# Softplus by ScalarE's own function, three of thirteen products with C from GpSimd to VectorE, and the program written out without loops

## The chip, the cores and the metric

The kernel runs on one core of a Trainium2 chip. The metric is the device time of one execution in microseconds (us). The engines are named as in the profile: PE (TensorE), DVE (VectorE), ACT (ScalarE), POOL (GpSimd) and SP, which only issues DMAs here.

## The reference

Four blocks follow one another on x (8 sequences of 512 positions, width 256): self and cross attention with a gated MLP, four Mamba layers, a cross attention with an MLP, and a last cross attention. The change touches the arithmetic of the Mamba layers alone. There 64 positions of context are put ahead of each sequence, so that 8 x 576 = 4608 positions run through every layer:

```python
def mamba_block(x, ip_w, cw, cb, xp_w, dtp_w, dtp_b, A_log, Dp, op_w):
    xi, z = jnp.split(jnp.einsum('bsd,ed->bse', x, ip_w), 2, axis=-1)      # 512 channels each
    xi = jax.nn.silu(conv4(xi) + cb)
    dt, Bm, Cm = jnp.split(jnp.einsum('bse,fe->bsf', xi, xp_w), [DR_, DR_ + DS_], axis=-1)
    dt = jax.nn.softplus(jnp.einsum('bsr,er->bse', dt, dtp_w) + dtp_b)
    A = -jnp.exp(A_log)                                                    # 512 x 16
    dA = jnp.exp(dt[..., None] * A)
    dBu = dt[..., None] * Bm[:, :, None, :] * xi[..., None]
    h = dA * h_before + dBu                  # along the sequence
    y = sum over the 16 states of (h * Cm)
    y = (y + xi * Dp) * jax.nn.silu(z)
    return jnp.einsum('bse,de->bsd', y, op_w)
```

All of it is float32.

## The kernel before

The activations stay in SBUF in `X`, channels on partitions. The stages run one after another: `self_attention`, cross attention, the gated MLP, `mamba`, a final norm, the second block, `last_attention`. Self attention and the two MLPs go over the eight sequences with `batches`, a hardware loop over seven of them and the last one written out. Each engine has its own loop, and semaphores alone order the engines. In a hardware loop every wait counts up to a number that the engine's sequencer works out in a register first.

`mamba` cuts the 4608 positions into 9 chunks of 512 columns, and so runs 4 x 9 = 36 steps. A hardware loop of two passes holds 18 steps each. A step works on 64 units. A unit is one 128 x 512 tile: 64 channels times two of the 16 states. Two units are a pair, j = 0 to 31, and eight pairs are a quarter k of the step (128 channels). For a pair:

- POOL multiplies dt*x with B for both units at once (L2586, 128 x 1024) into one of six places of `ring`. I call this the feed of pair j. It waits until the pair six before it has been summed by PE.
- ACT computes dA by Exp, one unit an instruction (L2554), into PSUM. Four PSUM banks hold two pairs, so ACT can be at most two pairs ahead of DVE. Before it reuses a place it saves the last column of h (L2173, L2177).
- DVE scans, h = dA*h + dBu, one unit an instruction (L2506).
- The product of h with C is done by DVE, one unit an instruction (`times_c`, L2304), or by POOL for both units (L2591). `BY_POOL` lists which pairs of each quarter are POOL's. POOL does such a product three pairs late: that of pair q follows the feed of pair q + 3.
- PE sums over the states with two products with `fold` (L2450), pair by pair in order.

Between the pairs stands the work that prepares the next step and finishes the last one, at fixed places: `late_pe` and `early_pe` on PE (convolution and projections, L2011, L2029, ...), `late_act` and `early_act` on ACT (copies out of PSUM, two Silu blocks after units 7 and 15, each between two table loads), `times_x` on POOL after the feeds of pairs 26 and 31 (dt*x), the gates on DVE (L2281). The last quarter of a step and the first one of the next hold most of PE's convolution, in order: halves of E1 and E2 at pairs 27 to 31, E3 at pairs 2 and 3. ACT takes E3 after unit 13, and Silu of all four follows after unit 15.

Softplus is not one instruction here. It is max(v, 0) + log(1 + exp(-|v|)), with a correction for rounding: `soft_begin` adds the bias, `soft_magnitude` and `soft_exponent` take Abs and Exp, and for each of four tiles t, `soft_log` writes 1 + e and its logarithm into two PSUM banks, and DVE finishes with three instructions (`soft_rest`, `soft_total`, `soft_finish`). These banks are those of the pairs, so each tile takes a pair's place in the order: after pairs 19, 21, 23 and 25 (`SOFT_AFTER`), 36 places a step in all.

## Time and profile before

| | |
|---|---|
| median of 3 runs | 6814.31 us |
| the runs | 6821.9, 6814.31, 6812.46 us |
| span of the profiled execution, first to last instruction | 6820.7 us |
| PE busy | 6141.5 us, 90% |
| DVE busy | 5101.9 us, 75% |
| POOL busy | 4645.4 us, 68% |
| ACT busy | 3775.4 us, 55% |
| mean granted TensorE clock | 0.946 |

The profile is of one execution, of span 6820.7 us; no other time of it is shown, and the highest of the three runs is 1.2 us above that span. Shares over the whole span mix stages with different limits. The Mamba steps take the stretch from 2057 to 6174 us of it, 60%.

### The profile page before, as it was taken

The page shows a single profiled execution, that of the slowest core. Times are in us where ns is not written, and L with a number is a line of the kernel's source. Part 1 is how long each engine was busy: PE and PEld are TensorE (multiplying, and loading weights), DVE is VectorE, ACT ScalarE, POOL GpSimd, SP SyncE. Part 2 cuts the span into 40 slices and gives each one's busy share as a digit, 9 for nine tenths or more (in the row PEclk, how much of TensorE's full clock was granted, in tenths as well). Part 3 has the DMA queues.
Part 4 walks back from the last instruction along what each step waited for, and adds up shares of the span by engine and source line. Part 5 has one row for each costly group of instructions (what it writes and reads, how often), then busy time and mean ns, then how long its engine had stood idle before and what let it go on. Part 6 is the DMA issues. An engine that isn't in the chain of part 4 may idle for free. (4 is left out here: it accounts for less than half of the span.)

```text
span 6820.7 us, 73597 instructions
## 1 busy us (share of the span) xinstructions
PE 6141.5 (90%) x20586; PEld 2578.2 (38%) x20586; DVE 5101.9 (75%) x5938; ACT 3775.4 (55%) x6915; POOL 4645.4 (68%) x2164
## 2 busy tenths in 40 slices
PE   9999999999999888989898989898888888888898
PEld 4555555444443333323232323232323232323444
DVE  4444555452219999999999999999999999995623
ACT  4444555432236666666666666666666666664432
POOL 3333444223009999999999999999999999993300
PEclk9999999999999898989898989998989999999998
DMA  2000000213003232323232323232333232332000
GB/s 78 0 0 0 0 0 0 83 31 112 0 7 90 68 82 67 95 68 90 61 90 60 93 71 93 60 89 62 87 79 90 63 87 63 87 79 56 5 0 25
DMA packets 228700, 387.50 MB, mean 57 GB/s; under 512 B 46305, under 2 KB 64417, under 8 KB 225937
## 3 DMA queue, kind: packets, MB, share of 16 engines
q1 hardware_dynamic: 228368, 383.75, 23.2%
q8 instruction: 126, 2.06, 0.1%
q14 instruction: 206, 1.68, 0.1%
HBM read 207.14 MB, written 23.40 MB: 34 GB/s over the span
## 5 line engine op out<-in xcount | busy, mean ns | idle before, releaser
L2586 POOL TENSOR_TENSOR work<-work,weights 128x1024 f32<-128x1024 f32 x1152 | 2692.4, 2364 | 15.5 <-PE banks L2450 7.2
L2450 PE MATMUL banks<-work 128*64 128x512 f32 x4608 | 1364.6, 674 | 549.8 <-POOL work L2591 549.3
L2506 DVE TENSOR_TENSOR_SCAN banks<-banks,work 128x512 f32<-128x512 f32 x1368 | 1712.2, 1273 | 41.7 <-ACT banks L2554 41.4
L2554 ACT ACTIVATE banks<-work 128x512 f32<-128x512 f32 x2304 | 1501.2, 680 | 68.6 <-DVE work L2298 43.2
L2506 DVE TENSOR_TENSOR_SCAN work<-banks,work 128x512 f32<-128x512 f32 x936 | 1174.9, 1271 | 98.1 <-ACT banks L2554 70.8
L2591 POOL TENSOR_TENSOR work<-work,weights 128x1024 f32<-128x1024 f32 x468 | 1104.2, 2359 | 159.0 <-ACT work L2173 159.0
L2011 PE MATMUL banks<-work,weights 128*128 128x512 f32 (+31 forms) x3796 | 1142.2, 451 | 3.6 <-DVE work L2271 3.0
L612 POOL TENSOR_TENSOR work<-work 128x1024 f32<-128x1024 f32 x256 | 480.0, 1895 | 743.3 <-DVE work L479 742.8
L2304 DVE TENSOR_TENSOR work<-banks,weights 128x512 f32<-128x512 f32 x1368 | 905.1, 673 | 0.0
L2011 PEld LDWEIGHTS banks<-work,weights 128*128 128x128 f32 x3796 | 634.6, 190 | 601.9 <-issue 523.3
L2450 PEld LDWEIGHTS banks<-work 128*64 128x64 f32 x4608 | 269.3, 144 | 1416.8 <-POOL work L2591 852.6
L2177 ACT ACTIVATE work<-banks 128x2 f32<-128x2 f32 x684 | 117.3, 171 | 1015.5 <-DVE work L2304 1011.3
L562 ACT ACTIVATE work<-banks,work 128x512 f32<-128x512 f32 x512 | 348.1, 690 | 201.1 <-DVE work L473 201.1
L473 DVE TENSOR_REDUCE work<-banks 128x2 f32<-128x1024 f32 x256 | 309.0, 1215 | 104.6 <-PE banks L398 104.6
L2029 PE MATMUL banks<-work,weights 128*128 128x512 f32 x592 | 352.9, 726 | 0.0
L1049 PE MATMUL banks<-work,weights 128*128 128x512 f32 x768 | 340.7, 598 | 11.4 <-ACT work L215 11.4
L463 DVE COPY work<-banks 128x512 f32<-128x512 f32 x256 | 175.9, 687 | 159.9 <-PE banks L388 159.9
L388 PE MATMUL banks<-ident,work 128*128 128x128 f32 x2048 | 277.8, 278 | 8.2 <-DVE work L463 4.7
L388 PEld LDWEIGHTS banks<-ident,work 128*128 128x128 f32 x2048 | 222.1, 141 | 151.7 <-issue 111.1
L398 PE MATMUL banks<-work 64*128 64x512 f32 x1024 | 254.4, 615 | 0.0
L375 PE MATMUL banks<-work 128*64 128x256 f32 x2048 | 247.5, 385 | 0.0
L1597 POOL TENSOR_TENSOR work<-work 128x512 f32<-128x512 f32 x8 | 11.2, 1416 | 322.7 <-ACT work L1712 322.7
(320 smaller groups left out, 7522.7 us busy)
## 6 DMA issues: line engine op xcount, KB each, us to landing
weights<-mamba_bc SPq DMA_DIRECT2D x592, 256.0 KB, 5.0
work<-work SPq DMA_DIRECT2D x1160, 128.0 KB, 2.3
weights<-mamba_taps SPq DMA_DIRECT2D x5, 2048.0 KB, 7.4
weights<-cross_vo SPq DMA_DIRECT2D x16, 512.0 KB, 6.9
mamba_taps<-work SPq DMA_DIRECT2D x4, 2048.0 KB, 6.5
cross_vo<-weights SPq DMA_DIRECT2D x6, 1024.0 KB, 9.2
work<-in_conv_rows SPq DMA_DIRECT2D x16, 256.0 KB, 6.6
out_T<-X SPq DMA_DIRECT2D x8, 512.0 KB, 3.3
```

The source lines that it names most:

```text
L388: mm = e.transpose(core.banks[:, 4 + j, kt * P:(kt + 1) * P], probs[:, 2 * (g % 2) + u, j, kt * P:(kt + 1) * P], core.ident[:])
L562: last = e.activation(probs[:, slot, j, :], core.banks[:, 2 * u + j, :], ACT.Exp, bias=nmax[:, slot, j:j + 1], accum_out=sums[:, slot, j:j ...
L612: e.tensor_tensor(probs[:, slot], probs[:, slot], rsum[:, slot, :].unsqueeze(2).to_broadcast([P, 2, T]), ALU.mult) \
L1049: mm = e.matmul(bank(i), w1[:, k, m * P:(m + 1) * P], normed[:, k, :], start=(k == 0), stop=(k == KD - 1))
L2011: mm = e.matmul(lane[:, a:b], conv_w[j][:, k, m * P:(m + 1) * P], nb[:, k, a + j:b + j], start=(d == 0 and k == 0), stop=(j == 0 and b == ...
L2029: mm = e.matmul(lane, z_w[:, k, m * P:(m + 1) * P], nb[:, k, TAPS - 1:], start=(k == 0), stop=(k == KD - 1))
L2304: last = e.tensor_tensor(ring_pair(n, j)[:, h, :], banks[:, slot_of(i), :], bc[:, j % SP_, 1, :], ALU.mult)
L2450: mm = e.matmul(ybank[k % 2][64 * h:64 * h + 64, :], fold, ring_pair(n, j)[:, h, :], start=False, stop=(a == SP_ - 1))
L2506: e.tensor_tensor_scan(ub if by_pool(j) else da, da, ub, state[:, i:i + 1], ALU.mult, ALU.add).then_inc(scanned, 1)
L2554: e.activation(banks[:, slot_of(i), :], dt_rep[:, k % 2, h, :], ACT.Exp, scale=decay[:, f:f + 1]).then_inc(da_full, 1)
L2586: e.tensor_tensor(ring_pair(n, j), u_rep[:, k % 2], bc[:, a, 0, :].unsqueeze(1).to_broadcast([P, 2, TC]), ALU.mult) \
L2591: e.tensor_tensor(ring_pair(n, q), ring_pair(n, q), bc[:, q % SP_, 1, :].unsqueeze(1).to_broadcast([P, 2, TC]), ALU.mult) \
```

## The change

Softplus becomes one function of ACT. `take_dt` reads PSUM as `soft_begin` did; for the first two tiles it still only adds the bias (after unit 37), for the last two, after unit 45, it applies Softplus at once, and `first_softplus` then turns the first two in one instruction of 1024 columns. A table load stands ahead of the block and one behind it, since Exp is in another table. The Abs, Exp, 1 + e and Ln instructions, the twelve DVE instructions and the four places in the PSUM banks go away. `BY_POOL` gives the products with C of pairs 10, 12, 18 and 22 to DVE and that of pair 11 to POOL: POOL has 10 a step where it had 13. Every hardware loop becomes a Python loop, so each step and each sequence has instructions of its own and constant numbers to wait for.

```diff
 def batches(e, body):
 
-    with e.Fori(0, B - 1) as b:
-        body(b, True)
-    body(B - 1, False)
-
-
...
-BY_POOL = ((0, 5), (0, 2, 4, 6), (0, 2, 4, 6), (0, 2, 4))
+BY_POOL = ((0, 5), (0, 3, 6), (0, 4), (0, 2, 4))
...
-SOFT_AFTER = (19, 21, 23, 25)
-STEP_GROUPS = PAIRS_N + KI
...
-    group_of = lambda j: j + sum(after < j for after in SOFT_AFTER)
-    soft_group = lambda t: SOFT_AFTER[t] + 1 + t
-    slot_of = lambda i: 2 * (group_of(i // 2) % 2) + i % 2
-    soft_slot = lambda t: 2 * (soft_group(t) % 2)
...
+    slot_of = lambda i: 2 * (i // 2 % 2) + i % 2
+    da_full_at = lambda N, i: val(N, UN, i + 1)
...
-    H_OUT, ABS_AT, EXP_AT = (37, 45), (38, 46), (39, 47)
-
-    def soft_begin(e, N, pair):
+    H_OUT = (37, 45)
+
+    def take_dt(e, N, pair, func):
 
         if N[1] >= 0:
             for s in range(2):
                 e.wait_ge(rep_in[s], rep_at(N, 2 * pair))
         ts, tv = ((0, 1), (3, 2))[pair]
         e.wait_ge(ln.s_full, s_at(N, f"H{ts}"))
-        e.activation(dt[:, ts, :], lane_s, ACT.Identity, bias=lv("dt_b", ts)).then_inc(ln.s_free, 1)
+        e.activation(dt[:, ts, :], lane_s, func, bias=lv("dt_b", ts)).then_inc(ln.s_free, 1)
         e.wait_ge(ln.v_full, v_at(N, f"H{tv}"))
-        e.activation(dt[:, tv, :], lane_v, ACT.Identity, bias=lv("dt_b", tv)).then_inc(ln.v_free, 1)
-
...
-        e.activation(u[:, 2 * pair:2 * pair + 2, :], dt[:, 2 * pair:2 * pair + 2, :], ACT.Abs).then_inc(magnitude, 1)
-
...
-        e.activation(u[:, at, :], u[:, at, :], ACT.Exp, scale=-1.0).then_inc(magnitude, 1)
...
-        e.activation(banks[:, b, :], u[:, t, :], ACT.Identity, bias=core.one[:, 0:1]).then_inc(da_full, 1)
-        e.wait_ge(da_full, soft_full_at(N, t, 1))
-        e.activation(banks[:, b + 1, :], banks[:, b, :], ACT.Ln).then_inc(da_full, 1)
...
+        e.activation(dt[:, tv, :], lane_v, func, bias=lv("dt_b", tv)).then_inc(ln.v_free, 1)
+
+    def first_softplus(e, N):
+
+        e.wait_ge(ln.s_free, s_at(N, "H0"))
+        e.wait_ge(ln.v_free, v_at(N, "H1"))
+        e.activation(dt[:, 0:2, :], dt[:, 0:2, :], ACT.Softplus).then_inc(first_dt, 1)
+
+    def slots_free(e, N, n, j):
+
+        M, j = (N, j - 2) if j >= 2 else (previous(N), PAIRS_N + j - 2)
+        m = n if M[1] == N[1] else n - 1
+        if N[1] >= 0 and by_pool(j):
...
-            if i == H_OUT[pair]:
-                soft_begin(e, N, pair)
-            if i == ABS_AT[pair]:
-                soft_magnitude(e, N, pair)
-            if i == EXP_AT[pair]:
-                soft_exponent(e, N, pair)
-        for t in range(KI):
-            if i == 2 * SOFT_AFTER[t] + 1:
-                soft_log(e, N, n, t)
+            if i == H_OUT[pair] and pair == 0:
+                take_dt(e, N, 0, ACT.Identity)
+            if i == H_OUT[pair] and pair == 1:
+                e.preload_act_table_set("softplus")
+                take_dt(e, N, 1, ACT.Softplus)
+                first_softplus(e, N)
+                e.preload_act_table_set("natural_log_exp_and_others")
...
-    def soft_rest(e, N, t):
-
-        e.wait_ge(da_full, soft_full_at(N, t, 2))
-        e.scalar_tensor_tensor(out=u[:, t, :], in0=banks[:, soft_slot(t), :], scalar=1.0, in1=u[:, t, :],
-                               op0=ALU.subtract, op1=ALU.subtract).then_inc(soft, 1)
-
-    def soft_total(e, N, t):
-
-        y = banks[:, soft_slot(t) + 1, :]
-        e.wait_ge(soft, soft_at(N, t, 1))
-        e.scalar_tensor_tensor(out=y, in0=y, scalar=log_1, in1=u[:, t, :], op0=ALU.subtract, op1=ALU.subtract).then_inc(soft, 1)
-
-    def soft_finish(e, N, t):
-
-        e.wait_ge(soft, soft_at(N, t, 2))
-        e.scalar_tensor_tensor(out=dt[:, t, :], in0=dt[:, t, :], scalar=0.0, in1=banks[:, soft_slot(t) + 1, :],
-                               op0=ALU.max, op1=ALU.add).then_inc(soft, 1)
...
-        e.wait_ge(soft, soft_at(N, 2 * pair + 1, 3))
+        if pair == 0:
+            e.wait_ge(first_dt, val(N, 1, 2))
+        else:
+            e.wait_ge(ln.s_free, s_at(N, "H3"))
+            e.wait_ge(ln.v_free, v_at(N, "H2"))
...
-            with e.Fori(0, LAYERS // 2) as l:
+            for l in range(LAYERS // 2):
```

On ACT, in the third quarter of a step, before the change. L2138 and L2140 read PSUM and add the bias, L2146 is Abs, L2152 Exp of the magnitude, L2554 the Exp of one unit; a REGISTER_ALU works out the number that a wait counts to. 1 + e and Ln (L2161, L2163) of each tile follow behind:

```order
L2554 ACTIVATE banks<-work 128x512 x2
L2137 REGISTER_ALU
L2138 ACTIVATE work<-banks,weights 128x512
L2140 ACTIVATE work<-banks,weights 128x512
L2170 REGISTER_ALU
L2554 ACTIVATE banks<-work 128x512
L2146 ACTIVATE work<-work 128x1024
L2554 ACTIVATE banks<-work 128x512
L2151 REGISTER_ALU
L2152 ACTIVATE work<-work 128x1024
L2157 REGISTER_ALU
L2172 REGISTER_ALU
```

After the change, the same place. L2119 and L2121 are now Softplus out of PSUM, L2127 is Softplus of the first two tiles, L2486 the Exp of a unit, L2135 and L2139 save a column:

```order
L2135 ACTIVATE work<-work 128x2
L2486 ACTIVATE banks<-work 128x512 x2
L2193 ACT_TABLE_LOAD
L2119 ACTIVATE work<-banks,weights 128x512
L2121 ACTIVATE work<-banks,weights 128x512
L2127 ACTIVATE work<-work 128x1024
L2196 ACT_TABLE_LOAD
L2139 ACTIVATE work<-banks 128x2
L2486 ACTIVATE banks<-work 128x512 x2
```

Five instructions now stand between the Exps of pair 22 and those of pair 23, where before single Exps stood between the pieces.

On DVE, before the change, the end of pair 21: both products with C, then the three instructions of one tile's softplus, then the next scans (which this list calls SCALAR_TENSOR_TENSOR, like the softplus ones; L2506 is the scan):

```order
L2506 SCALAR_TENSOR_TENSOR banks<-banks,work 128x512
L2511 REGISTER_ALU
L2304 TENSOR_TENSOR work<-banks,weights 128x512
L2514 REGISTER_ALU
L2304 TENSOR_TENSOR work<-banks,weights 128x512
L2285 REGISTER_ALU
L2286 SCALAR_TENSOR_TENSOR work<-banks,work 128x512
L2292 REGISTER_ALU
L2293 SCALAR_TENSOR_TENSOR banks<-banks,work 128x512
L2297 REGISTER_ALU
L2298 SCALAR_TENSOR_TENSOR work<-work,banks 128x512
```

After the change, from the second scan of pair 19 to pair 21 (L2441 is the scan, L2246 the product with C, L2241 a gate):

```order
L2241 TENSOR_TENSOR work<-banks,work 128x512
L2441 SCALAR_TENSOR_TENSOR banks<-banks,work 128x512
L2246 TENSOR_TENSOR work<-banks,weights 128x512
L2441 SCALAR_TENSOR_TENSOR work<-banks,work 128x512
L2246 TENSOR_TENSOR work<-banks,weights 128x512
L2441 SCALAR_TENSOR_TENSOR work<-banks,work 128x512
L2441 SCALAR_TENSOR_TENSOR banks<-banks,work 128x512 x2
L2246 TENSOR_TENSOR work<-banks,weights 128x512
```

The softplus instructions are gone, and so are the register instructions; scans and products follow one another directly.

## Rows read from the trace of the kernel before

**Rows 1.** Windows, all 36 steps: length, busy us (instructions) an engine, PEclk, DMA share, GB/s.

```profile
2057.01:6173.84 4116.83, 3567.05 (x10555) 1298.28 (x10554) 3969.62 (x4319) 2669.03 (x4792) 3938.56 (x1771) 0.92 0.33 78
```

**Rows 2.** Windows, the four quarters of the third step (order: PE, PEld, DVE, ACT, POOL).

```profile
2286.49:2315.80 29.31, 29.31 (x106) 13.94 (x106) 26.26 (x29) 23.32 (x36) 27.37 (x12) 1.00 0.41 90
2315.80:2341.30 25.50, 20.61 (x56) 6.33 (x55) 25.50 (x28) 14.39 (x30) 23.04 (x11) 0.93 0.14 32
2341.30:2372.50 31.20, 23.40 (x56) 5.72 (x54) 30.99 (x37) 22.80 (x41) 31.20 (x15) 0.78 0.15 34
2372.50:2400.78 28.28, 26.01 (x96) 13.32 (x94) 27.49 (x32) 13.71 (x28) 28.08 (x15) 1.00 0.60 144
```

**Rows 3.** Waits, 2057 to 6174 us: who waited for whom, us in total, times, longest.

```profile
DVE work L2506 <- ACT banks L2554: 70.8, 36, 2.4
...
DVE banks L2506 <- ACT banks L2554: 41.4, 39, 2.3
...
DVE work L2506 <- POOL work L2586: 27.2, 35, 7.0
```

**Rows 4.** Timeline, DVE, third quarter of the third step: start, us, instruction.

```profile
2351.91 1.28 DVE L2506 TENSOR_TENSOR_SCAN banks<-banks,work 128x512 f32<-128x512 f32 x1
2353.10 1.27 DVE L2304 TENSOR_TENSOR work<-banks,weights 128x512 f32<-128x512 f32 x2
2354.28 0.68 DVE L2286 SCALAR_TENSOR_TENSOR work<-banks,work 128x512 f32<-128x512 f32 x1
...
2356.40 2.45 DVE L2506 TENSOR_TENSOR_SCAN work<-banks,work 128x512 f32<-128x512 f32 x2
```

**Rows 5.** Timeline, POOL, third step: feeds 24 and 25, products 22 and 26.

```profile
2364.86 4.68 POOL L2586 TENSOR_TENSOR work<-work,weights 128x1024 f32<-128x1024 f32 x2
2369.50 2.36 POOL L2591 TENSOR_TENSOR work<-work,weights 128x1024 f32<-128x1024 f32 x1
...
2385.98 2.37 POOL L2591 TENSOR_TENSOR work<-work,weights 128x1024 f32<-128x1024 f32 x1
```

**Rows 6.** Timeline, PE: sum of pair 26, and the second half of E3.

```profile
2388.41 1.08 PE L2450 MATMUL banks<-work 128*64 128x512 f32 x4 [1.23 <-POOL work L2591]
...
2418.50 3.71 PE L2011 MATMUL banks<-work,weights 128*128 128x256 f32 x16
```

**Rows 7.** Timeline, ACT: the Silu block after unit 15 of the fourth step.

```profile
2424.23 1.28 ACT L2217 ACT_TABLE_LOAD   x1
2425.53 1.91 ACT L2217 ACTIVATE work<-work 128x2048 f32<-128x2048 f32 x1
2427.45 1.28 ACT L2218 ACT_TABLE_LOAD   x1
2428.75 0.17 ACT L2177 ACTIVATE work<-banks 128x2 f32<-128x2 f32 x1
2428.95 1.30 ACT L2554 ACTIVATE banks<-work 128x512 f32<-128x512 f32 x2
```

**Rows 8.** Timeline, DVE: the scan behind that block, unit 16.

```profile
2429.68 1.28 DVE L2506 TENSOR_TENSOR_SCAN work<-banks,work 128x512 f32<-128x512 f32 x1 [1.61 <-ACT banks L2554]
```

**Rows 9.** Timeline, ACT: bias, Exp of a unit and Abs in the third step.

```profile
2363.86 0.67 ACT L2138 ACTIVATE work<-banks,weights 128x512 f32<-128x512 f32 x1
...
2365.00 0.69 ACT L2554 ACTIVATE banks<-work 128x512 f32<-128x512 f32 x1
2365.62 1.05 ACT L2146 ACTIVATE work<-work 128x1024 f32<-128x1024 f32 x1
```

**Rows 10.** Timeline, DVE: the first scan of each of the loop's two passes.

```profile
2057.01 2.46 DVE L2506 TENSOR_TENSOR_SCAN work<-banks,work 128x512 f32<-128x512 f32 x2 [7.03 <-POOL work L2586]
...
4120.38 2.46 DVE L2506 TENSOR_TENSOR_SCAN work<-banks,work 128x512 f32<-128x512 f32 x2 [5.64 <-POOL work L2586]
```

**Rows 11.** Timeline, PE, self attention, one of the loop's boundaries.

```profile
306.74 1.17 PE L388 MATMUL banks<-ident,work 128*128 128x128 f32 x8 [0.44 <-POOL work L612]
...
318.33 1.07 PE L388 MATMUL banks<-ident,work 128*128 128x128 f32 x8 [0.60 <-DVE work L463]
```

More of the change, by code:

```diff
@@ L239, in batches @@
 def batches(e, body):
-    with e.Fori(0, B - 1) as b:
-        body(b, True)
-    body(B - 1, False)
-def batches_apart(e, body):
-    body(0, False, True)
-    with e.Fori(1, B - 1) as b:
-        body(b, True, True)
-    body(B - 1, True, False)
+    for b in range(B):
+        body(b, b < B - 1)
 UNITS = 2
@@ L607, in _ @@
         def _(e):
-            with e.Fori(0, B) as b:
+            for b in range(B):
                 for n in range(H0 * UNITS):
@@ L1762, in layer_of @@
 def layer_of(a, layer):
-    return a[bass.ds(layer, 1)].rearrange("l r n -> (l r) n")
+    return a[layer]
 def tiled(a, layer):
@@ L1963, in mamba @@
     bc_ready = [S(f"bc_ready{a}") for a in range(SP_ // 2)]
-    u_done, kept, saved, magnitude, soft = S("u_done"), S("kept"), S("saved"), S("magnitude"), S("soft")
+    u_done, kept, saved = S("u_done"), S("kept"), S("saved")
     rep_in = [S("rep_in0"), S("rep_in1")]
     da_full, fed, scanned, prod_d, prod_q, summed = S("da_full"), S("fed"), S("scanned"), S("prod_d"), S("prod_q"), S("summed")
-    gated = S("gated")
+    gated, first_dt = S("gated"), S("first_dt")
     y_full, y_free, y_added = S("y_full"), S("y_free"), S("y_added")
@@ L1972, in mamba @@
     q_index = lambda j: sum(by_pool(i) for i in range(j))
-    group_of = lambda j: j + sum(after < j for after in SOFT_AFTER)
-    soft_group = lambda t: SOFT_AFTER[t] + 1 + t
-    slot_of = lambda i: 2 * (group_of(i // 2) % 2) + i % 2
-    soft_slot = lambda t: 2 * (soft_group(t) % 2)
-    in_group = {group_of(j): (j, None) for j in range(PAIRS_N)} | {soft_group(t): (None, t) for t in range(KI)}
-    da_full_at = lambda N, i: val(N, 2 * STEP_GROUPS, 2 * KI + 1 + 2 * group_of(i // 2) + i % 2 + 1)
-    soft_full_at = lambda N, t, d: 1 + 2 * t + d if N[1] == -1 else val(N, 2 * STEP_GROUPS, 2 * KI + 1 + 2 * soft_group(t) + d)
-    soft_at = lambda N, t, d: val(N, 3 * KI, 3 * KI + 3 * t + d)
+    slot_of = lambda i: 2 * (i // 2 % 2) + i % 2
+    da_full_at = lambda N, i: val(N, UN, i + 1)
     fed_at = lambda N, j: val(N, PAIRS_N, j + 2)
@@ L2424, in _ @@
             e.matmul(ybank[1], core.ident[:], z[:, 1, 0, :], start=True, stop=True).then_inc(summed, 1)
-            with e.Fori(0, LAYERS // 2) as l:
+            for l in range(LAYERS // 2):
                 for n in range(BODIES):
@@ L2475, in _ @@
             for i in range(UN):
-                for t in range(KI):
-                    if i == 2 * SOFT_AFTER[t] + 2:
-                        soft_rest(e, (0, -1), t)
-                        soft_total(e, (0, -1), t)
-                        soft_finish(e, (0, -1), t)
                 early_dve(e, (0, -1), i, -1, normed[:, 1])
-            with e.Fori(0, LAYERS // 2) as l:
+            for l in range(LAYERS // 2):
                 for n in range(BODIES):
@@ L2496, in _ @@
                             gate(e, previous(N), KI - 1, z[:, (n + 1) % 2])
-                        for t in range(KI):
-                            if j == SOFT_AFTER[t] + 1 and h == 0:
-                                soft_rest(e, N, t)
-                                soft_total(e, N, t)
-                                soft_finish(e, N, t)
                         if h == 0:
@@ L2506, in _ @@
                         e.tensor_tensor_scan(ub if by_pool(j) else da, da, ub, state[:, i:i + 1], ALU.mult, ALU.add).then_inc(scanned, 1)
-                        if h == 0 and j > 0 and j - 1 not in SOFT_AFTER and not by_pool(j - 1):
+                        if h == 0 and j > 0 and not by_pool(j - 1):
                             e.wait_ge(scanned, scanned_at(N, i - 1))
@@ L2512, in _ @@
                             times_c(e, N, n, j, 0)
-                        if h == 1 and (j in SOFT_AFTER or j == PAIRS_N - 1) and not by_pool(j):
+                        if h == 1 and j == PAIRS_N - 1 and not by_pool(j):
                             e.wait_ge(scanned, scanned_at(N, i))
@@ L2526, in _ @@
             e.wait_ge(set_up, SET_UP)
-            e.activation(scrap[:, 16:17], zero, ACT.Copy).then_inc(da_full, 1)
-            e.activation(log_1, core.one[:, 0:1], ACT.Ln)
             e.wait_ge(core.middle_loaded, MIDDLE_LOAD)
@@ L2535, in _ @@
                 early_act(e, (0, -1), i, -1, x[:, 1], normed[:, 1], normed[:, 0])
-            e.wait_ge(soft, soft_at((0, -1), KI - 1, 3))
-            with e.Fori(0, LAYERS // 2) as l:
+            for l in range(LAYERS // 2):
                 for n in range(BODIES):
@@ L2574, in _ @@
                 times_x(e, (0, -1), pair, x[:, 0], 0)
-            with e.Fori(0, LAYERS // 2) as l:
+            for l in range(LAYERS // 2):
                 for n in range(BODIES):
@@ L2600, in _ @@
                         bound_decay(e)
-SET_UP = 5
+SET_UP = 4
 def final_norm(core):
```

23 lines of the change are left out of this document (1 added, 22 removed).

## The prediction

> **What bounds the kernel now.** I first read the windows over all Mamba steps: 4116.83 us for 36 steps, 114.4 us each, in which DVE is busy for 3969.62 us (110.3 a step), POOL for 3938.56 (109.4), PE for 3567.05 (99.1) and ACT for 2669.03 (74.1) [rows 1]. So DVE and POOL are both within 5 us of the step, and PE within 15. No engine can be shortened alone. The waits say what fills DVE's missing 4 us: dA of ACT is late 75 times, 112 us in all, and a feed of POOL 35 times, 27 us [rows 3]. The quarters of one step show where each engine is tight [rows 2]. In the first PE is busy without a gap (29.31 of 29.31). In the second DVE is (25.50 of 25.50). In the third both DVE and POOL are (30.99 and 31.20 of 31.20). In the fourth POOL has 28.08 of 28.28 and DVE 27.49.
>
> One chain runs through the fourth quarter and the next step's first. POOL's feed of pair 24 ends at about 2367.2 (the first of the two in 2364.86 to 2369.50), then comes the product of pair 22, and so on without a gap to the product of pair 26, which starts at 2385.98 and ends at 2388.35 [rows 5]. PE has waited for it, starts at 2388.41, and from there works without a gap until the last half of E3 ends at 2422.21 [rows 6]. ACT takes E3 and Exp of pair 7, then Silu between two table loads, and the first Exp of pair 8 starts at 2428.95 [rows 7]; DVE scans unit 16 at 2429.68 after waiting 1.61 [rows 8]. From the first scan of the fourth quarter (2372.44) to that scan are 57.2 us, and DVE's own work in it is 27.49 + 26.26 = 53.8 [rows 2]. The other two quarters are DVE's own pace.
>
> **The change, part by part.**
>
> Softplus on DVE. The two products of a pair start at 2353.10 and the first softplus instruction at 2354.28: 0.59 us each from start to start. The three softplus instructions last from there to the next scan at 2356.40: 2.12 us a tile, three tiles in the third quarter and one in the fourth, 8.5 us a step [rows 4]. All of it goes. Scans go at 1.19 us each (2351.91 to 2353.10).
>
> The products. Four pairs come to DVE and one leaves it: two more instructions in the second quarter and four in the third, 6 x 0.59 = 3.5 us. DVE's sum is 8.5 - 3.5 = 4.9 us a step less: 105.4. POOL loses three at 2.32 us from start to start (two feeds take from 2364.86 to 2369.50 [rows 5]), 7.0 us: 102.4 a step. POOL stops being as tight as DVE; that pays only because DVE falls too.
>
> ACT. Four additions of one, four Ln, two Abs and two Exp of 1024 columns leave, two table loads and one Softplus of 1024 come. ACT has 40 us to spare a step [rows 1], so its sum costs nothing; what counts is that the new instructions stand in one block after unit 45 while DVE goes on. The trace has no Softplus. From below I take the additions that it replaces: two out of PSUM take from 2363.86 to 2365.00, 1.14 us, and Abs of 1024 columns 1.05 us [rows 9]. Silu, another function from another table, takes 1.91 us for 2048 columns, 0.93 a thousand [rows 7], so functions do not differ much here, and I take these values. A load costs 1.30 us from its start to the next start (2424.23 to 2425.53 [rows 7]). The block is 1.30 + 1.14 + 1.05 + 1.30 = 4.8 us. From above, three Softplus at twice the time make it 7.0.
>
> What the block delays: the Exps of pair 23. I count from the end of pair 20's second scan, which is what frees its places. DVE then has four scans of pairs 21 and 22 and three products before it wants unit 46: 4 x 1.19 + 3 x 0.59 = 6.5 us. ACT at that time still has 0.4 us of the Exps of pair 21, then a saved column and two Exps (0.11 + 1.28), the block (4.8), a saved column and one Exp (0.9, by the step from 2428.75 to 2429.68 [rows 7, 8]): 7.5. DVE waits 0.9 to 1.0 us, a new wait in each step; with the upper bound 3.1. Behind the block stand only the Exps and copies of the next units, and ACT is ahead again one pair later. POOL's first dt*x stands after the feed of pair 26 and finds its softplus done about 4 us earlier.
>
> On this block the Trainium skill speaks against the change. The traced loads follow the instruction ahead of them and are followed by the next one within 0.02 us [rows 7]. The skill's page ScalarE: Activation LUTs, section What ACT_TABLE_LOAD costs, gives each switch a drain of about 1.38 us besides the 1.28 of the load. By that rule the block would be an estimated 2.8 us longer and DVE's wait 3.7.
>
> The chain. Its part on POOL loses the product of pair 22, 2.3 us; PE's part and ACT's part stay word for word. The stretch of 57.2 us falls to 54.9. POOL comes into the fourth quarter 5.3 us ahead (2367.2 against 2372.44) [rows 4, 5]; with POOL lighter than DVE in the second and third quarter that lead grows until the product of pair 20, which follows that pair's scan, holds it. From the end of that scan to the fourth quarter DVE has pairs 21 to 23 and the new wait, 6 x 1.19 + 6 x 0.59 + 0.95 = 11.6 us, POOL the product of pair 20 and the feed of pair 24, 4.6, and ACT's saved column ahead of them, 0.3: a lead of 6.6 us at most, 1.3 more than now. I take some 0.5 of it: 54.4. DVE's own work there is 53.8 - 2.1 = 51.7, so 2.7 us of waits are left where there were 3.4.
>
> The step: 54.4 for these two quarters; 25.5 + 1.2 = 26.7 for the second; 31.2 - 6.4 + 2.4 + 0.95 = 28.2 for the third. Together 109.3, where the third step has 114.3 [rows 2]. That is 5.0 a step, or as DVE's 4.9 with waits unchanged in sum (0.7 less in the chain, 0.95 new). I take 4.9: 36 x 4.9 = 176 us.
>
> No loops. At the second pass DVE's first scan waited 5.64 us for POOL [rows 10]. The waits for POOL other than those two first scans are 27.2 - 7.0 - 5.6 = 14.6 over 33 steps, 0.4 each, so the boundary cost about 5 us; some of that lead is regained after it, and I take 3.5. Before the first scan (7.03 us of wait [rows 10]) softplus stands on the way; it gets shorter by the DVE part, but PE's projections end there too: I take 3. In self attention PE has two gaps at a boundary, 0.44 and 0.60 us [rows 11]; nothing shows how much of them is the loop. Seven boundaries: 0 to 7 us, I take 4. The register instructions are not busy time and lie under it in the Mamba steps, since scans follow at 1.19 us with them. Table loads, DMAs and products elsewhere stay.
>
> The sum: 176 + 3.5 + 3 + 4 = 187 us. From the profiled execution, 6820.7 us of span and about a microsecond around it, that leaves 6635; the median stands 7.6 us under the highest run, so 6628 us, 2.7% less.
>
> **The rivals.**
>
> PE takes over. It has 99.1 us a step whatever happens [rows 1], and in the fourth and first quarter 26.01 + 29.31 = 55.3 of 57.6 [rows 2]. If its order ahead of pair 26 is as binding as behind it, losing the product of pair 22 helps nothing and these quarters stay at 57.2: the step is 57.2 + 26.7 + 28.2 = 112.1, the gain 2.2 x 36 = 79, the time about 6725. Against it: PE waited 1.23 us just before that pair [rows 6], and its clock is at the lower of its two levels for a part of the third quarter only (0.78 on average, with 1.00 in the fourth [rows 2]). 14%.
>
> Softplus is slow. With the upper bound of 7.0 us for the block the new wait is 3.1 and not 0.9: 2.2 x 36 = 79 us more, 6707. 8%.
>
> The switch is dear: into and out of Softplus's table ACT stands still for another load's length each time, 1.3 us, where around Silu it did not. That is 2.6 x 36 = 94 us more, 6722. The rows of Silu speak against it [rows 7], so 5%. This is the drain of the skill's page on ScalarE, whose own figure makes it an estimated 100 us.
>
> Waits vanish with POOL's slack: DVE waits 112.2 / 36 = 3.1 us a step for ACT now [rows 3]. If the lead makes good 1.8 of it, a step is 107.5 and the time 6565. 6%.
>
> Slower than before. One mechanism could do it: Softplus as a function that ACT runs far below the pace of Silu. The gain of 4.9 us a step is gone when the new wait reaches 5.8 us, the block 9.7, so when its three Softplus instructions take 7.1 us instead of 2.2, 3.2 times as long. At four times a step costs 1.7 us more than now and the time is about 6865. All of ACT's functions in these rows keep to about 0.93 us a thousand columns, so 4%.
>
> The change does nothing for the time, because softplus on DVE had been covered: DVE has no gap in the third quarter [rows 2], so this is the least likely, 2%.
>
> **How the numbers follow.** The forecast has 61%, PE as bound 14%, the slow function 8%, the dear switch 5%, the better case 6%, slower 4%, the same 2%. What a measurement of this kernel can tell from no change is about 0.2%, 14 us. Only the last two cases are not faster by more. The likeliest case's own range is 6600 to 6660. The range of 8 in 10 goes down to 6585, halfway to the case without waits, and up to 6715, which takes in the slow function and most of the way to PE as the bound.
>
> **What would show it.** A step of about 109.3 us; DVE busy about 105.4 and POOL 102.4 a step; Softplus of 1024 columns at about 1.05 us and of 512 at 0.7, the block 4.8 us; a wait of about 1 us of DVE for ACT at unit 46, and those at units 8 and 16 nearly as before; POOL's waits for PE small. The forecast is wrong if the fourth and first quarter still take 57 us together, if the wait at unit 46 is above 2 us, or if the parts outside the Mamba steps change by more than 10 us.

## The result, and the profile after

The changed kernel takes 6637.85 us (median of 4 runs, 6635.33 to 6641.31), where the kernel before takes 6818.1 (4 runs). The ratio is 0.9737 with the interval 0.9725 to 0.9749: 2.6% faster. The forecast was 6628 us, within 6585 to 6715. The profiled execution has a span of 6635.5 us and is the run of 6637.25 us.

From the page of the changed kernel, the first rows (busy us, share of the span, instructions):

```profile
span 6635.5 us, 60648 instructions
...
PE 6113.6 (92%) x20586; PEld 2570.3 (39%) x20586; DVE 4926.2 (74%) x5709; ACT 3566.2 (54%) x6568; POOL 4394.1 (66%) x2056
```

Windows of the changed kernel, in the columns of [rows 1, 2]: all 36 steps, then the second step, then the first quarter of the third step.

```profile
2053.49:5997.33 3943.84, 3549.53 (x10574) 1298.23 (x10574) 3804.57 (x4103) 2482.41 (x4469) 3687.54 (x1663) 0.92 0.35 81
2169.12:2278.19 109.07, 97.47 (x306) 37.05 (x304) 105.66 (x115) 69.01 (x124) 102.40 (x47) 0.92 0.33 78
2278.19:2306.80 28.61, 28.61 (x104) 13.83 (x103) 26.20 (x29) 22.86 (x35) 26.29 (x12) 1.00 0.37 82
```

The steps take 3943.84 us instead of the 4116.83 of [rows 1], 173.0 less. A step inside a layer takes 109.1; the mean over all, with the first step and the ends of layers, is 109.6. DVE is busy for 105.66 us of a step and POOL for 102.40. The quarters' medians are 28.6, 26.7, 27.7 and 26.0 us.

The timeline of ACT around the new block, changed kernel, third step (start, us, instruction). L2193 and L2196 are the table loads, L2119, L2121 and L2127 Softplus:

```profile
2350.58 1.28 ACT L2486 ACTIVATE banks<-work 128x512 f32<-128x512 f32 x2
2351.88 1.28 ACT L2193 ACT_TABLE_LOAD   x1
2353.17 0.69 ACT L2119 ACTIVATE work<-banks,weights 128x512 f32<-128x512 f32 x1
2353.76 0.68 ACT L2121 ACTIVATE work<-banks,weights 128x512 f32<-128x512 f32 x1
2354.33 1.06 ACT L2127 ACTIVATE work<-work 128x1024 f32<-128x1024 f32 x1
2355.40 1.28 ACT L2196 ACT_TABLE_LOAD   x1
2356.70 0.17 ACT L2139 ACTIVATE work<-banks 128x2 f32<-128x2 f32 x1
```

The block runs from 2351.88 to 2356.70, 4.82 us. Softplus has the pace of the other functions, and the next instruction starts 0.02 us behind a load. The wait that the block makes is on DVE at unit 46 (timeline, same step):

```profile
2356.02 0.67 DVE L2246 TENSOR_TENSOR work<-banks,weights 128x512 f32<-128x512 f32 x1
2357.69 1.29 DVE L2441 TENSOR_TENSOR_SCAN banks<-banks,work 128x512 f32<-128x512 f32 x1 [1.00 <-ACT banks L2486]
```

The waits of the changed kernel from 2160 to 5990 us, as in [rows 3]:

```profile
DVE banks L2441 <- ACT banks L2486: 75.5, 76, 1.1
DVE work L2441 <- ACT banks L2486: 52.2, 35, 2.4
...
ACT work L2167 <- PE banks L1992: 9.8, 7, 1.6
```

DVE's waits are 128 us over some 35 steps, 3.6 a step: 0.99 at unit 46, 1.1 at unit 8 and 1.5 at unit 16 on average. None is for POOL any more. The last row is ACT waiting for E3, which is late in 7 of the 35 steps here; it becomes important below.

What was not seen before the experiments, and explains most of them, is a circle in the kernel **before**: an event that leads to itself one step later. The rows are the timeline of the kernel before, third and fourth step, POOL, PE, ACT, POOL. L2591 is the product with C of pair 8, L2062 the output projection that finishes the step before, whose result goes to X, L2187 its copy:

```profile
2320.93 2.36 POOL L2591 TENSOR_TENSOR work<-work,weights 128x1024 f32<-128x1024 f32 x1 [2.46 <-ACT work L2173]
...
2430.46 3.60 PE L2062 MATMUL banks<-work,weights 128*128 128x512 f32 x8
...
2434.09 0.60 ACT L2187 ACTIVATE X<-banks 128x512 f32<-128x512 f32 x1 [0.52 <-PE banks L2062]
2434.59 0.20 ACT L2173 ACTIVATE work<-work 128x2 f32<-128x2 f32 x1
...
2434.86 2.35 POOL L2591 TENSOR_TENSOR work<-work,weights 128x1024 f32<-128x1024 f32 x1 [2.44 <-ACT work L2173]
```

From 2320.93 POOL works without a gap until the product of pair 26 ends at 2388.35 [rows 5]: 29 instructions of 2.32 us. PE starts at 2388.41 [rows 6] and works without a gap to 2434.06. ACT copies, saves a column of pair 8, and the product of pair 8 starts again at 2434.86, 113.9 us after 2320.93. That is the step, and no instruction of DVE is in it. I call it the POOL-PE circle. Ten products with C lie in it before (pairs 8 to 26), seven after. Less three products of 2.32 us, an estimated 106.9 us would be left.

### The profile page after: what moved, and what is told of

Read it like the earlier page. It is cut to its first block and busy times, and to the rows that moved or that the text cites. A ratio compares the mean times of both kernels' runs of the same rounds, so it can differ in the third digit from the quotient of the medians.

```text
span 6635.5 us, 60648 instructions
## 1 busy us (share of the span) xinstructions
PE 6113.6 (92%) x20586; PEld 2570.3 (39%) x20586; DVE 4926.2 (74%) x5709; ACT 3566.2 (54%) x6568; POOL 4394.1 (66%) x2056
## 5 line engine op out<-in xcount | busy, mean ns | idle before, releaser
L2518 POOL TENSOR_TENSOR work<-work,weights 128x1024 f32<-128x1024 f32 x1152 | 2684.8, 2359 | 17.3 <-PE banks L2396 6.7
L2441 DVE TENSOR_TENSOR_SCAN banks<-banks,work 128x512 f32<-128x512 f32 x1584 | 1984.8, 1271 | 85.0 <-ACT banks L2486 84.1
L2396 PE MATMUL banks<-work 128*64 128x512 f32 x4608 | 1344.8, 665 | 394.3 <-POOL work L2523 268.6
L2486 ACT ACTIVATE banks<-work 128x512 f32<-128x512 f32 x2304 | 1495.7, 680 | 25.5
L1992 PE MATMUL banks<-work,weights 128*128 128x512 f32 (+31 forms) x3796 | 1141.5, 451 | 3.0 <-DVE work L2231 3.0
L2246 DVE TENSOR_TENSOR work<-banks,weights 128x512 f32<-128x512 f32 x1584 | 1055.5, 668 | 0.0
L2523 POOL TENSOR_TENSOR work<-work,weights 128x1024 f32<-128x1024 f32 x360 | 847.6, 2354 | 237.6 <-ACT work L2135 237.6
L2441 DVE TENSOR_TENSOR_SCAN work<-banks,work 128x512 f32<-128x512 f32 x720 | 911.0, 1269 | 78.4 <-ACT banks L2486 78.4
L1992 PEld LDWEIGHTS banks<-work,weights 128*128 128x128 f32 x3796 | 634.7, 190 | 600.6 <-issue 524.3
L2139 ACT ACTIVATE work<-banks 128x2 f32<-128x2 f32 x792 | 136.3, 172 | 1328.3 <-DVE work L2246 1326.4
L464 DVE TENSOR_REDUCE work<-banks 128x2 f32<-128x1024 f32 x256 | 308.8, 1214 | 105.1 <-PE banks L389 104.7
L1040 PE MATMUL banks<-work,weights 128*128 128x512 f32 x768 | 343.0, 601 | 9.6 <-ACT work L215 9.6
L2010 PE MATMUL banks<-work,weights 128*128 128x512 f32 x592 | 341.9, 706 | 0.0
L322 PE MATMUL banks<-work,weights 128*128 128x512 f32 x512 | 224.9, 597 | 5.7 <-ACT work L215 4.2
```

The costliest lines, as they stand in the source:

```text
L1040: mm = e.matmul(bank(i), w1[:, k, m * P:(m + 1) * P], normed[:, k, :], start=(k == 0), stop=(k == KD - 1))
L1992: mm = e.matmul(lane[:, a:b], conv_w[j][:, k, m * P:(m + 1) * P], nb[:, k, a + j:b + j], start=(d == 0 and k == 0), stop=(j == 0 and b == ...
L2010: mm = e.matmul(lane, z_w[:, k, m * P:(m + 1) * P], nb[:, k, TAPS - 1:], start=(k == 0), stop=(k == KD - 1))
L2246: last = e.tensor_tensor(ring_pair(n, j)[:, h, :], banks[:, slot_of(i), :], bc[:, j % SP_, 1, :], ALU.mult)
L2396: mm = e.matmul(ybank[k % 2][64 * h:64 * h + 64, :], fold, ring_pair(n, j)[:, h, :], start=False, stop=(a == SP_ - 1))
L2441: e.tensor_tensor_scan(ub if by_pool(j) else da, da, ub, state[:, i:i + 1], ALU.mult, ALU.add).then_inc(scanned, 1)
```

## The experiments

Ratios are against the kernel before on the same chip. The windows below go from the first to the last scan of the Mamba steps, 36 steps, with the columns of [rows 1]. In e1 and e2 the scan is L2505, in the others L2441 (e5 and e11 L2439, e6 L2443). `BY_POOL` of the changed kernel is ((0, 5), (0, 3, 6), (0, 4), (0, 2, 4)).

**e1, the kernel before without loops.**

```diff
-            with e.Fori(0, LAYERS // 2) as l:
+            for l in range(LAYERS // 2):
```

The same is done at every loop of the Mamba steps and, with the matching code, at `batches` and the loop of POOL in self attention.

> The kernel before with its loops written out and nothing else changed. By the prediction's terms (one boundary of the Mamba loop 3.5 us, seven of self attention 0 to 7 us) it takes 6807 to 6815 us where the kernel before takes 6818. The rival, that a longer straight program costs time at the instruction side, gives more than 6822 us.

6813.06 us, ratio 0.9996 (0.9987 to 1.0005). The loops by themselves make no difference that can be measured in the time of the whole. In the traces the boundary shows a little: the step across it and the next one last 119.3 and 112.7 us in the kernel before, 115.0 and 114.6 here, 2.3 us less together.

```profile
2056.11:6170.98 4114.87, 3562.13 (x10562) 1300.10 (x10560) 3972.10 (x4319) 2669.41 (x4792) 3935.84 (x1771) 0.93 0.33 78
```

**e2, the changed kernel with the old softplus** (e1 with the new `BY_POOL`).

```diff
-BY_POOL = ((0, 5), (0, 2, 4, 6), (0, 2, 4, 6), (0, 2, 4))
+BY_POOL = ((0, 5), (0, 3, 6), (0, 4), (0, 2, 4))
```

> The kernel after with the softplus of before (12 DVE instructions a step, its four places in the banks); loops are written out and POOL has 10 products. If DVE's sum decides the step, DVE has 110.3 + 3.5 = 113.8 us of work and 3 us of waits: 116.5 to 117.5 a step, 6885 to 6930 us in all, slower than before. If POOL decided the step before, its 7 us less give a step of 114 or less and a time of 6815 or less.

6904.09 us, ratio 1.0126 (1.011 to 1.0141), slower. The three products alone, with the loops written out, cost 1.3%. DVE is busy for 4095.03 of 4202.89 us, 113.8 a step, and a step inside a layer takes 116.5: with three products more on DVE, DVE decides. Less the 3.5 us of these products, DVE's own circle (its work and its waits behind ACT) is an estimated 113.0 us in the kernel before, 0.9 behind the POOL-PE circle.

```profile
2058.59:6261.48 4202.89, 3604.67 (x10566) 1307.67 (x10566) 4095.03 (x4535) 2675.39 (x4792) 3694.78 (x1663) 0.90 0.31 76
```

**e3, the changed kernel with the old BY_POOL.** The new softplus and no loops, nothing else.

```diff
-BY_POOL = ((0, 5), (0, 3, 6), (0, 4), (0, 2, 4))
+BY_POOL = ((0, 5), (0, 2, 4, 6), (0, 2, 4, 6), (0, 2, 4))
```

> The kernel after with the 13 products of POOL as before. If DVE's sum alone decides, a step is 109.1 - 3.5 = 105.6 us and the time 6512 us. If POOL takes over, its 109.4 us of work and 1 to 2 us of waits decide: 110.4 to 111.5 a step, 6685 to 6725 us. I expect the second.

6816.2 us, ratio 0.9999 (0.999 to 1.0008). This lies above both expectations, and it changed my view: DVE is free for 11 us of each step, POOL for 4.6, and no gain shows. The windows of e3, all steps and one step:

```profile
2054.01:6168.78 4114.77, 3552.02 (x10566) 1298.39 (x10566) 3692.83 (x3887) 2475.02 (x4469) 3932.90 (x1768) 0.93 0.33 78
2287.33:2401.16 113.83, 98.19 (x306) 38.83 (x304) 102.54 (x108) 68.70 (x124) 109.22 (x50) 0.93 0.32 75
```

The stretch is that of e1 to 0.1 us, since the POOL-PE circle is the same. The 8 us that DVE is given come back as waits: 4.2 us at unit 46, and for POOL's feeds 1.8 at unit 0 and 0.5 to 1.0 each at units 44, 56 and 60 (the last row below). Those at units 8 and 16, 0.9 and 2.2, are about what they were before. The waits of e3, from 2160 us on:

```profile
DVE banks L2441 <- ACT banks L2486: 171.4, 70, 4.3
DVE work L2441 <- POOL work L2518: 100.0, 100, 3.0
```

**e4, eleven products, in other places.** Pairs 19 and 22 are POOL's and pair 20 is not.

```diff
-BY_POOL = ((0, 5), (0, 3, 6), (0, 4), (0, 2, 4))
+BY_POOL = ((0, 5), (0, 3, 6), (0, 3, 6), (0, 2, 4))
```

> The kernel after with 11 products of POOL: pairs 0, 5, 8, 11, 14, 16, 19, 24, 26, 28 and 22 in place of 20. If DVE's work plus the waits behind ACT's three table blocks decide the step, it falls by 1.2 us to 107.9, 6595 us. If the chain through POOL's products, PE and the Silu decides (product of pair 22 back in the fourth quarter), it rises by up to 2.3 us a step, up to 6720 us; if both are level, the time stays at 6638 us.

6781.18 us, ratio 0.9949 (0.9934 to 0.9964). Four fifths of the gain are lost with one product more: a step of 112.8 us, where DVE works for 104.8 and POOL for 104.7. The timelines of e4, ACT and POOL, third step, show how (L2135 saves a column of a pair of POOL's, L2523 is the product of pair 22):

```profile
2357.76 0.17 ACT L2139 ACTIVATE work<-banks 128x2 f32<-128x2 f32 x1 [3.32 <-DVE work L2246]
...
2359.28 1.28 ACT L2193 ACT_TABLE_LOAD   x1
...
2362.81 1.28 ACT L2196 ACT_TABLE_LOAD   x1
...
2365.54 0.19 ACT L2135 ACTIVATE work<-work 128x2 f32<-128x2 f32 x1
...
2365.81 2.35 POOL L2523 TENSOR_TENSOR work<-work,weights 128x1024 f32<-128x1024 f32 x1 [2.77 <-ACT work L2135]
```

ACT waits for pair 20's products on DVE before it can go on to the block, and the column that POOL needs for pair 22 is saved behind the block. So POOL stands 2.77 us and then has work without a gap to pair 26: a third path, from DVE over the block into POOL's last stretch. It closes into a circle as well: DVE scans unit 16 at 2313.17 and works without a gap to the products of pair 20, and behind POOL's product of pair 26 come PE to E3, the Silu block and unit 16 of the next step at 2426.01, 112.84 us later. Unit 46 waits 2.6 us as well. The time is outside what I expected, and the sums of the engines do not show why.

**e5, Abs in place of Softplus, no loads.** Softplus is left out of the computation.

```diff
-        e.activation(dt[:, 0:2, :], dt[:, 0:2, :], ACT.Softplus).then_inc(first_dt, 1)
+        e.activation(dt[:, 0:2, :], dt[:, 0:2, :], ACT.Abs).then_inc(first_dt, 1)
...
-                e.preload_act_table_set("softplus")
-                take_dt(e, N, 1, ACT.Softplus)
+                take_dt(e, N, 1, ACT.Abs)
...
-                e.preload_act_table_set("natural_log_exp_and_others")
```

> The kernel after with Abs in the place of Softplus and without the two table loads around it; softplus is thus left out of the computation. The block behind unit 45 shrinks from 4.8 to 2.2 us, and DVE's wait at unit 46 (0.99 us) goes. If DVE's work and its waits behind ACT decide the step (109.1 us), it falls to 108.1 and the time to 6602 us. If the chain through POOL, PE and the Silu decides, nothing changes: 6638 us.

6630.69 us, ratio 0.9725 (0.9711 to 0.974). The wait at unit 46 is gone (0.99 us), but the step is shorter by 0.3 only, 108.8. What was gained is lost at unit 16, which waits 2.1 us on average instead of 1.5: E3 of PE is now late in every step. The time lies between the two that I expected. The waits of e5:

```profile
DVE work L2439 <- ACT banks L2484: 74.7, 35, 2.4
...
ACT work L2167 <- PE banks L1992: 33.9, 35, 2.3
```

So a second path stands 0.3 us behind DVE's pace in the changed kernel. I call it the mixed path: scan of pair 20 on DVE, its product on POOL, POOL without a gap to the product of pair 26, PE to E3, ACT's Silu block, the scan of unit 16, and DVE's own work back to pair 20 of the next step. I count 43.95 us for DVE's part, from the scan of unit 16 to the start of POOL's product of pair 20, and 64.85 for the rest over POOL, PE and ACT to the next scan of unit 16: 108.8. The rows of e8 below show both.

**e6, two more table loads ahead of the block.**

```diff
                 e.preload_act_table_set("softplus")
+                e.preload_act_table_set("natural_log_exp_and_others")
+                e.preload_act_table_set("softplus")
```

> The kernel after with two more table loads in the Softplus block, which is 2.6 us longer (7.4 us). If DVE's wait at unit 46 is on the path, it goes from 1.0 to 3.6 us and the step to 111.7, 6730 us. If the slack ahead of the fourth quarter takes it up, less than half of that shows: under 6685 us.

6763.61 us, ratio 0.992 (0.9905 to 0.9935). The two loads make the block 2.58 us longer, and unit 46 waits 3.57 us instead of 0.99: 2.58 more, with no further delay around a switch. The timelines of e6, ACT and DVE:

```profile
2355.96 1.28 ACT L2193 ACT_TABLE_LOAD   x1
2357.25 1.28 ACT L2194 ACT_TABLE_LOAD   x1
2358.54 1.28 ACT L2195 ACT_TABLE_LOAD   x1
2359.83 0.69 ACT L2119 ACTIVATE work<-banks,weights 128x512 f32<-128x512 f32 x1
...
2364.35 1.29 DVE L2443 TENSOR_TENSOR_SCAN banks<-banks,work 128x512 f32<-128x512 f32 x1 [3.58 <-ACT banks L2488]
```

The whole is dearer than the wait: 3.4 us a step (4066.79 us for the steps, 122.9 more than the changed kernel) and not 2.6, and the time is above what I expected. The steps vary between 111.7 and 115.9 us. The trace shows where the other 0.8 us come in. DVE's longer wait at unit 46 keeps PE waiting too, for 2 to 3.5 us instead of 0.5, and behind that PE's twelve products for the convolution (L1992) are not always at the same speed. PE's timeline in two steps that follow one another:

```profile
2366.28 1.08 PE L2398 MATMUL banks<-work 128*64 128x512 f32 x4 [3.24 <-DVE work L2248]
2367.29 5.40 PE L1992 MATMUL banks<-work,weights 128*128 128x512 f32 x12
...
2478.64 1.08 PE L2398 MATMUL banks<-work 128*64 128x512 f32 x4 [3.11 <-DVE work L2248]
2479.65 3.71 PE L1992 MATMUL banks<-work,weights 128*128 128x512 f32 x12
```

The granted clock is 0.73 in the first stretch (window 2366.28 to 2372.60) and 1.00 in the second (2478.64 to 2483.29). Behind the fast one unit 16 waits 1.28 us, as it mostly does in the changed kernel, and from one unit 16 to the next it takes 111.66 us: 109.08 and the 2.58 of the two loads. Behind the slow one PE is 1.7 us later, E3 is late, unit 16 waits 1.98, and it takes 112.53. It is so through the whole trace: the seven steps of 111.66 us all have a fast stretch, the slow ones take from 112.1 to 116.3, and E3 is late in 26 steps instead of 7. So the rest comes in with PE, at the lower granted clock behind a longer wait. I made no run that changes this alone.

**e7, one DVE instruction moved into the block's shadow.** The gate that stood ahead of unit 39 on DVE goes to unit 45, so that DVE has 0.6 us more to do while ACT is in the block.

```diff
-                            if i == 16 * (f + 1) + 7:
+                            if i == (23, 45, 55)[f]:
```

> The kernel after with DVE's second gate (0.6 us) moved from ahead of unit 39 to ahead of unit 45, so that DVE has it to do while ACT is in the Softplus block. If DVE's work and waits add up to the step, the wait at unit 46 falls from 1.0 to 0.4 us and the time by 0.6 x 36 = 21 us to 6617. If the chain decides, or PE is held up by the later gate, it is 6638 us or more.

6623.96 us, ratio 0.9709 (0.9695 to 0.9722). Unit 46 waits 0.40 us and a step takes 108.5, the 0.6 us of the gate less. The 36 steps take 3925.0 us, 18.8 less than in the changed kernel, where I had given 21.

**e8, eleven products, with that of pair 4.** It lies outside both the POOL-PE circle and the mixed path, and takes two instructions off DVE.

```diff
-BY_POOL = ((0, 5), (0, 3, 6), (0, 4), (0, 2, 4))
+BY_POOL = ((0, 4, 5), (0, 3, 6), (0, 4), (0, 2, 4))
```

> The kernel after with the product with C of pair 4 on POOL too, 11 a step. Read from the traces so far, the loop that set the step of before is: product of pair 8, then POOL without a gap to the product of pair 26, then PE without a gap to the last product of the residual, then ACT's copy and saved column, then the product of pair 8 again. Pair 4 lies outside of it, where POOL waits 2.2 us for pair 5. DVE has 1.2 us less to do: 107.9 a step, 6596 us. If what counts is POOL's number of products (11 gave 6781 us with pairs 19 and 22), it is near 6780 us.

6630.33 us, ratio 0.9724 (0.9711 to 0.9738). Neither expected time came: DVE's pace would have been 107.9; the step is 108.8 as in e5, unit 16 waits 2.2 us, and E3 is late in every step. By another way than e5, the step stops at the same number: that is the mixed path's. The timelines of e8 along it, third step: DVE's scan of unit 16, POOL's product of pair 20, PE's sum of pair 26, ACT taking E3, the next scan of unit 16:

```profile
2306.70 1.28 DVE L2441 TENSOR_TENSOR_SCAN work<-banks,work 128x512 f32<-128x512 f32 x1 [2.21 <-ACT banks L2486]
...
2350.64 2.35 POOL L2523 TENSOR_TENSOR work<-work,weights 128x1024 f32<-128x1024 f32 x1 [1.00 <-ACT work L2135]
...
2374.17 1.08 PE L2396 MATMUL banks<-work 128*64 128x512 f32 x4 [0.50 <-POOL work L2523]
...
2408.01 0.69 ACT L2167 ACTIVATE work<-banks,weights 128x512 f32<-128x512 f32 x1 [1.88 <-PE banks L1992]
...
2415.52 1.28 DVE L2441 TENSOR_TENSOR_SCAN work<-banks,work 128x512 f32<-128x512 f32 x1 [2.21 <-ACT banks L2486]
```

The waits of e8:

```profile
DVE work L2441 <- ACT banks L2486: 116.4, 70, 2.4
ACT work L2167 <- PE banks L1992: 78.1, 35, 3.8
```

**e9, thirteen products as before, one of them moved.** Pair 22 goes from POOL to DVE and pair 4 from DVE to POOL, against e3.

```diff
-BY_POOL = ((0, 5), (0, 2, 4, 6), (0, 2, 4, 6), (0, 2, 4))
+BY_POOL = ((0, 4, 5), (0, 2, 4, 6), (0, 2, 4), (0, 2, 4))
```

> The kernel of the run with 13 products of POOL (6816 us, 113.86 a step) with one of them moved: pair 4 in place of pair 22. POOL's and DVE's sums stay as they were. By the loop read from the traces (product of pair 8, POOL without a gap to the product of pair 26, PE without a gap to the residual, ACT's saved column, product of pair 8), one POOL instruction of 2.3 us leaves the loop: 111.5 a step and 6732 us. If POOL's total of 13 products decides, it stays at 6816 us.

6730.31 us, ratio 0.9871 (0.9856 to 0.9886). The busy times of DVE, ACT and POOL are those of e3 to 5 us over the whole stretch, the steps take 82.8 us less, 2.3 each: one product of 2.32 us fewer in the POOL-PE circle. This is the test of the circle, since the place of one product is all that changed.

```profile
2052.68:6084.68 4032.00, 3551.73 (x10570) 1302.92 (x10571) 3688.14 (x3887) 2470.10 (x4469) 3930.73 (x1770) 0.92 0.34 79
```

**e10, e7 and e8 together.** The diffs are those of both.

> Two edits together: the product of pair 4 on POOL (11 a step) and DVE's second gate ahead of unit 45. DVE's work and waits come to 108.5 - 1.2 = 107.3 us a step. The path scan of pair 20, its product on POOL, on to that of pair 26, PE to E3, Silu, scan of unit 16 and DVE on to pair 20 came to 108.8 with the gate in it and 108.2 without. I expect 108.2 a step: 6612 us, a little under the run with the gate alone (6624). If DVE alone decides: 6580 us.

6615.81 us, ratio 0.97 (0.9687 to 0.9714), a step of 108.2. It is the lowest time of the kernels that compute everything, 0.3% under the changed one. Against e7 the intervals of the two ratios overlap; the step, 108.2 against 108.5, is what tells them apart.

**e11, e5 with pair 26's product on DVE and pair 4's on POOL.** It takes 2.3 us off the mixed path. Softplus is left out here too (Abs in its place, no loads).

```diff
-BY_POOL = ((0, 5), (0, 3, 6), (0, 4), (0, 2, 4))
+BY_POOL = ((0, 4, 5), (0, 3, 6), (0, 4), (0, 4))
```

> The kernel with Abs in the place of Softplus (softplus left out of the computation, no table loads there; 108.8 us a step, 6631 us) with the product of pair 26 given to DVE and that of pair 4 to POOL: 10 products as before, DVE's sum unchanged. If the path through POOL's product of pair 26 and PE holds that kernel at 108.8, it is now shorter by 1 to 2 us and DVE's own work and waits decide: 108.1 a step, 6605 us. If DVE's work was already what held it, it stays at 6631 us.

6594.85 us, ratio 0.967 (0.9655 to 0.9685), a step of about 107.9. With the wait at unit 46 gone and the mixed path shortened, the step falls below the 108.8 at which e5 and e8 stood, to about DVE's work and its other waits (109.1 less 0.99). This is what shows that the mixed path held e5.

**e12, three products early in the step.** e7's gate, and POOL has pairs 3, 4 and 5 in the first quarter but not 26.

```diff
-BY_POOL = ((0, 5), (0, 3, 6), (0, 4), (0, 2, 4))
+BY_POOL = ((0, 3, 4, 5), (0, 3, 6), (0, 4), (0, 4))
```

> The kernel after with DVE's second gate ahead of unit 45, and 11 products of POOL: pairs 0, 3, 4, 5, 8, 11, 14, 16, 20, 24, 28. The path through POOL's product of pair 26 is gone, as in the run with Abs. DVE has 1.2 us less than with the gate alone (108.5), but pair 3's product leaves the stretch that covers the Silu block, so the wait at unit 8 grows by up to 0.6: 107.9 us a step, 6603 us, against 6616 for the best so far. If PE, which takes the fourth and first quarter without a gap, decides, it stays at 108.2 and 6616 us.

6696.72 us, ratio 0.9821 (0.9808 to 0.9835), a clear miss. Three products close together on POOL, with one feed between each, make PE wait in the first quarter, where it had no gap [rows 2]. PE's projection into X is late for it, ACT's copy too, and DVE's unit 20 behind that. The timelines of PE and DVE in e12, and one row of its waits, with L2149 the copy into X and L2043 the projection:

```profile
2305.24 1.08 PE L2396 MATMUL banks<-work 128*64 128x512 f32 x4 [2.67 <-POOL work L2523]
...
2319.41 1.29 DVE L2441 TENSOR_TENSOR_SCAN banks<-banks,work 128x512 f32<-128x512 f32 x1 [3.79 <-ACT banks L2486]
...
ACT X L2149 <- PE banks L2043: 117.4, 35, 4.3
```

The second quarter is 30.4 us long in the median instead of 26.7, and the steps take 110.2 or 111.8 to 111.9 us. The two kinds differ by PE's clock: from this wait to the end of the first projection into X (L2034) it takes 7.3 us at a granted clock of 0.76 in the step shown, and 5.6 us at 1.00 in the next one, which is one of 110.2. Moving work out of a full engine did not pay here, because it landed in front of another that is full there.

## Why the prediction was right, and where it was not

**The steps.** The sum for DVE was right, term by term. The block was put at 4.8 us and takes 4.82, Softplus of 512 and 1024 columns at 0.7 and 1.05 and takes 0.69 and 1.06, the new wait at 0.9 to 1.0 and is 0.99. DVE was to be at 105.4 and POOL at 102.4; they are at 105.66 and 102.40. The fourth and the first quarter were to take 54.4 and take 54.6, the step 109.3 and takes 109.1. From the first sum of PE to its last one (2069.5 to 6186.7 us before, 2070.0 to 6008.7 after) the steps lost 178.5 us, where 176 + 3.5 were given; from DVE's first scan to its last, 173.0.

**Two engines bound it: wrong.** The first paragraph of the prediction read from the busy sums that DVE and POOL were both tight, and the second took the second and third quarter for DVE's own pace. The kernel before was bound by one thing, the POOL-PE circle of 113.9 us; e3 shows that 8 us a step less on DVE give nothing, and e9 that a single product out of the circle gives its 2.3. DVE's own circle was close behind, an estimated 113.0, and e2 shows that it takes over when products go from POOL to DVE. What the prediction drew from this, that neither engine can be shortened alone, held. The gain therefore belongs to neither part: softplus alone 0.9999, the products alone 1.0126, both 0.9737. The forecast came out right because with both parts DVE's circle does decide (109.1, against 108.8 of the mixed path and 106.9 of the POOL-PE circle), and it was DVE's work and waits that I added up. That was partly luck, by 0.3 us a step: the prediction had closed neither of the other two into a circle, and had the mixed path been a microsecond longer, the sum would have given a time that is too low.

**The rival given 2%** said that softplus on DVE had been covered, and was put aside because DVE has no gap in the third quarter. For this part alone it was true (e3). An engine without a gap in one quarter had its slack in the others, and what a quarter saves comes back as a wait later in the step.

**PE as bound** (14%, 6725) did not come true: the first quarter, with PE busy for all of its 28.61 us, shrank with the rest. PE is in both circles, behind POOL's last product, and only there. **The dear switch** (5%): by the Trainium skill, ScalarE: Activation LUTs, What ACT_TABLE_LOAD costs, each switch has a drain of about 1.38 us besides the load. The traces do not agree: 0.01 to 0.02 us before and behind each load, and in e6 two loads add 2.58 us to the wait. **Waits vanish** (6%): e5 shows why not, the mixed path is next after 0.3 us.

**The parts outside the steps.** The profiled execution got shorter by 185.2 us where the terms add up to 187. By the windows of [rows 1] 173.0 of them are steps, 3.5 come before the first scan and 8.7 after the last one. That is 12.2 outside them, more than the 10 us that the prediction named as a sign of being wrong; its sum had 3 + 4 = 7 for them. So the total is better than its terms. The 3.5 us for the boundary of the loop lie within what e1 can tell (3.3 us less, interval from 8.9 less to 3.4 more); its trace has 2.3. The 3 us ahead of the first scan gave nothing to the end: DVE's first scan starts 3.5 us earlier, 2053.49 against 2057.01 [rows 10], but that pair's sum on PE comes 0.5 us later, because PE's projections end there as the prediction itself said. Of the 4 us in self attention 0.5 to 0.8 came, and 1.8 up to the end of the MLP. The last attention, whose code is the same, took 5.7 us less; here windows of the kernel before and of the changed one over the same part of it:

```profile
6765.00:6780.00 15.00, 12.45 (x58) 11.00 (x58) 5.08 (x7) 3.76 (x6) 2.96 (x2) 0.61 0.14 51
```

```profile
6585.50:6600.50 15.00, 13.33 (x69) 8.40 (x68) 8.80 (x13) 3.70 (x6) 2.94 (x2) 0.89 0.14 53
```

The granted clock is 0.61 in one and 0.89 in the other. Two windows alone say too much, though: in the four windows of 15 us from 6735 it is 0.81, 0.85, 0.61 and 0.73 before, in the four from 6555.5 it is 0.89, 0.77, 0.89 and 0.60 after. The low stretch comes later, and the mean is 0.79 instead of 0.75. That much is seen; I made no run on it, and part of it is within the few microseconds by which runs of one kernel differ. It goes the other way to the terms that fell short, so the total is nearer to the forecast than its small terms are.

**The last term.** The sum took 7.6 us off because the profiled run of the kernel before was at the top of its runs. The profiled run of the changed kernel is not (6637.25 us, median 6637.85). Most of the 10 us between 6628 and the measured time is this term.

## What to carry to other kernels

Before costing a change to a pipelined loop, take one event and follow what released it back until the same event of the step before: the length of that circle is the step, and an engine that is 96% busy may not be in it. Then look for the next circles, because in the changed kernel three lay within 3 us of each other and each gain stopped at the next one (e5, e8). Ask of each piece of work not how much it loads its engine but whether it lies in the circle: one product moved out of it at unchanged loads gave 1.3% (e9), three products close together where another engine was full gave back about 80 us of e10's gain of about 205 (e12), and one instruction moved under a block of another engine gave all of its 0.6 us (e7).
